# Expert tiles of 128 slots, two to a job, second weights kept in SBUF

## The reference, cut to what matters

```python
logits = einsum('btd,ed->bte', x, w_router); probs = softmax(logits)
vals, idx = top_k(probs, 2)                       # gates
hs  = gelu(x @ Ws1.T + bs1);  acc = hs @ Ws2.T + bs2       # shared
h   = gelu(einsum('btd,efd->btef', x, W1) + b1)            # 8 experts, F = 512
y   = einsum('btef,edf->bted', h, W2) + b2
out = SCALE * (acc + einsum('bted,bte->btd', y, gates))
```

## Time and profile before

| | us |
|---|---|
| median of 3 runs | 635.91 |
| lowest and highest run | 635.18, 636.79 |
| the profiled execution, its time | 635.87 |
| the profiled execution, its span | 634.1 |
| PE busy | 570.1 (90%) |
| DVE, ACT, POOL busy | 443.8, 333.6, 391.1 |

### The profile page before, as it was taken

One profiled execution on the slowest core, in us unless ns is written; L12 is line 12 of the kernel. 1 busy time (PEld: TensorE's weight loads), 2 busy tenths in 40 slices (PEclk: granted clock), 3 DMA queues, 4 the chain that ended last, 5 costly groups with the idle time before them and its releaser, 6 DMA issues. The chain is left out here.

```text
span 634.1 us, 14426 instructions
## 1 busy us (share of the span) xinstructions
PE 570.1 (90%) x4296; PEld 512.1 (81%) x4296; DVE 443.8 (70%) x1743; ACT 333.6 (53%) x1064; POOL 391.1 (62%) x598
## 2 busy tenths in 40 slices
PE   2469999999999999999996868789979999999993
PEld 2349999899999999999985557778869999999991
DVE  3736888888788888878886478884595465555765
ACT  2555666566566666656662374775434444444440
POOL 1525666656666665666652607888888886677760
PEclk9999999999999999999999768879999999999997
DMA  9079930000000000000000001145445577778945
GB/s 198 3 275 394 395 136 1 2 0 0 0 0 0 0 0 0 0 0 0 2 2 1 2 0 35 46 143 168 143 137 147 177 222 225 227 239 256 347 123 165
DMA packets 39796, 66.77 MB, mean 105 GB/s; under 512 B 7522, under 2 KB 26724, under 8 KB 39748
## 3 DMA queue, kind: packets, MB, share of 16 engines
q1 hardware_dynamic: 31076, 54.85, 27.4%
q0 software_dynamic: 4544, 9.45, 4.3%
q10 hardware_dynamic: 4128, 1.91, 1.4%
HBM read 36.26 MB, written 29.92 MB: 104 GB/s over the span
## 5 line engine op out<-in xcount | busy, mean ns | idle before, releaser
L1586 ACT ACTIVATE hid<-bank,slab 128x256 f32<-128x256 f32 x156 | 64.1, 470 | 85.1 <-PE bank L1442 85.0
L2052 POOL DMA_INDIRECT ys<-yo,dst x78 | 76.3, 979 | 36.8 <-DVE yo L1922 22.2
L2044 POOL DMA_INDIRECT xs<-hrow,slot_i x64 | 63.4, 990 | 35.8 <-issue 35.5
L1442 PE MATMUL bank<-hg,slab 128*128 128x256 f32 x312 | 73.9, 380 | 4.3 <-issue 3.9
L1456 PEld LDWEIGHTS bank<-slab,hid 128*128 128x128 f32 x624 | 75.8, 192 | 2.0
L1456 PE MATMUL bank<-slab,hid 128*128 128x128 f32 x624 | 76.0, 275 | 0.0
L1442 PEld LDWEIGHTS bank<-hg,slab 128*128 128x128 f32 x312 | 56.3, 190 | 11.0 <-issue 4.9
L1917 DVE TENSOR_TENSOR yb<-bank,slab 128x256 f32<-128x256 f32 x39 | 16.6, 424 | 61.9 <-PE bank L1456 61.7
L990 POOL TENSOR_TENSOR nL<-aL,ones 128x128 f32<-128x128 bf16 x32 | 16.9, 527 | 42.5 <-ACT aL L699 42.5
L413 PE MATMUL bank<-aH,W2p 128*128 128x128 f32 x192 | 42.4, 303 | 0.1
L413 PE MATMUL bank<-kv,W1b 128*128 128x128 f32 x192 | 41.4, 298 | 0.0
(11 more groups left out here) (353 smaller groups left out, 1882.4 us busy)
## 6 DMA issues: line engine op xcount, KB each, us to landing
slab<-in_slabs_dram SPq DMA_DIRECT2D x39, 578.0 KB, 3.8
xs<-fill SPq DMA_DIRECT2D x34, 528.0 KB
xt<-xs SPq DMA_DIRECT2D x39, 132.0 KB, 3.2
yg<-ys SPq DMA_DIRECT2D x8, 512.0 KB, 6.7
xr<-in_L_attn_x_dram SPq DMA_DIRECT2D x16, 128.0 KB, 7.0
ys<-yo,dst POOLq DMA_INDIRECT x78, 3.1
xs<-hrow,slot_i POOLq DMA_INDIRECT x64
out_dram<-xr SPq DMA_DIRECT2D x16, 64.0 KB, 2.9
```

The source lines that it names most:

```text
L1442: mm = pe.matmul(e_half(i, n), left[:, n * P:(n + 1) * P], right, start=True, stop=True)
L1586: nc.scalar.activation(hid[i % 2][:, n, :], e_half(i, n), ACT.Gelu_apprx_tanh, bias=bias).then_inc(e_x, 1)
L2044: pool.indirect_dma_start(out=xs[:, :], out_offset=bass.IndirectOffsetOnAxis(ap=slot_i[:, i, c:c + 1], axis=0), in_=hrow[:, c, :], in_offs ...
L2052: pool.indirect_dma_start(out=ys[:, :], out_offset=bass.IndirectOffsetOnAxis(ap=dst[v][:, s:s + 1], axis=0), in_=yo[v][:, s, :], in_offset ...
```

## The change

A tile has 128 slots (`HALF`), and a job takes two tiles that may belong to different experts. 64 full tiles and up to 7 part empty ones, made even, give 72 tiles or `N_TILES` = 36 jobs; `N_FULL` becomes 12. There are then 43 jobs in all: expert jobs 0 to 11 with four shared tiles among the first eight, a shared tile, expert jobs 12 to 35, two shared tiles. `e_up` has eight products of 128 columns instead of four of 256, and `e_gelu` eight pieces of 128. The second weights of all experts are loaded once (`w2`, 2 MB) and addressed in `e_down` through a register that TensorE loads itself. A slab has 644 numbers per partition and a job needs two; the ring is `RW` = 4. SyncE issues two slab DMAs and two row DMAs per job; it derives the expert from the row's register by a shift (an expert's region has 4096 rows), so a slab needs no register load of its own, except for the first ones (`early_weights`). `hid` shares the buffers of `hs`. The tables have 72 entries, and the grids behind them are finer.

```diff
-SLAB = 2 * F + FT + D
-N_TILES = (2 * B * S) // TS + E - 1
+SLAB = F + FT + D
+HALF = P
+N_HALVES = -(-((2 * B * S) // HALF + E - 1) // SUB) * SUB
+N_TILES = N_HALVES // SUB
-N_FULL = -(-(B * S - E * (TS - 1)) // TS)
+N_FULL = -(-(B * S - E * (HALF - 1)) // HALF) // SUB
-RW = 5
+RW = 4
@@ SyncE
-                def weights(j):
+                def weights(j, experts):
                     if j >= RW:
                         sp.wait_ge(e_yb, job["expert", j - RW] + 1)
-                    e = sp.value_load(e_i[0:1, j:j + 1], min_val=0, max_val=E - 1)
-                    sp.dma_start(slab[j % RW][:, :], slabs[:, bass.ds(e, 1), :].rearrange("p o w -> p (o w)")).then_inc(s_slab[j % RW], 16)
+                    for s in range(SUB):
+                        sp.dma_start(slab[j % RW][:, s, :], slabs[:, bass.ds(experts[s], 1), :].rearrange("p o w -> p (o w)")).then_inc(s_slab[j % RW], 16)
+                def early_weights(j):
+                    weights(j, [sp.value_load(e_i[0:1, SUB * j + s:SUB * j + s + 1], min_val=0, max_val=E - 1) for s in range(SUB)])
...
+                    at = [sp.value_load(row_i[0:1, SUB * j + s:SUB * j + s + 1], min_val=0, max_val=XS_ROWS - HALF) for s in range(SUB)]
+                    for s in range(SUB):
+                        sp.dma_start(xt[j % RX][:, s, :], xs[bass.ds(at[s], HALF), :]).then_inc(s_xt[j % RX], 16)
+                    return at
+                sp.dma_start(w2[:, :, :], e_w2).then_inc(s_w2, 16)
...
+                    at = rows(j)
                     if j >= RW:
-                        weights(j)
+                        weights(j, [a >> 12 for a in at])
                 sp.wait_ge(table_ready, 4)
-                weights(N_FULL)
-                weights(N_FULL + 1)
+                early_weights(N_FULL)
+                early_weights(N_FULL + 1)
@@ TensorE, e_up and e_down
+                        if kind == "expert":
+                            for s in range(SUB):
+                                mm = pe.matmul(e_half(i, n)[:, s * P:(s + 1) * P], slab[j % RW][:, s, n * P:(n + 1) * P],
+                                               hg[j % 2][:, s * P:(s + 1) * P], start=True, stop=True)
...
+                        expert = [pe.value_load(e_i[0:1, SUB * j + s:SUB * j + s + 1], min_val=0, max_val=E - 1) for s in range(SUB)]
...
-                            right = slab[j % RW][:, F + n * P:F + (n + 1) * P] if kind == "expert" else sw[:, 1, n, :]
+                            right = w2[:, bass.ds(expert[s], 1), n * P:(n + 1) * P].rearrange("p o w -> p (o w)") if kind == "expert" else sw[:, 1, n, :]
@@ DVE, meta
-                    dve.scalar_tensor_tensor(out=row2[:, :], in0=xt[r][:, :, D + 1], scalar=e, in1=xt[r][:, :, D],
-                                             op0=ALU.not_equal, op1=ALU.add)
+                    dve.tensor_tensor(other[:, :], xt[r][:, :, D + 1], etab[:, SUB * j:SUB * (j + 1)], ALU.not_equal).then_inc(meta_step, 1)
+                    dve.wait_ge(meta_step, 2 * j + 1)
+                    dve.tensor_tensor(row2[:, :], other[:, :], xt[r][:, :, D], ALU.add)
```

More of the change, by code:

```diff
@@ L132, in program @@
         at = 0
-        for name, width in (("iota", E), ("down", E), ("tri", E * E), ("step", CAP // TS), ("tile", N_TILES), ("tau", CH), ("dump", SUB * RY), ("b2row", D)):
+        for name, width in (("iota", E), ("down", E), ("tri", E * E), ("step", CAP // HALF), ("tile", N_HALVES), ("tau", CH), ("dump", SUB * RY), ("b2row", D)):
             cut[name] = tabs[:, at:at + width]
@@ L1215, in program @@
             held, marks = psb("held", [P, 3, E]), psb("marks", [P, 4 * E])
-            over = psb("over", [P, E, CAP // TS])
+            over = psb("over", [P, E, CAP // HALF])
             tri = psb("tri", [P, 3 * E, E])
-            past = psb("past", [P, N_FULL, E])
+            past = psb("past", [P, FULL, E])
             full, number, weight = psb("full", [P, E]), psb("number", [P, 3 * E]), psb("weight", [P, 3 * E])
-            first, rowf = psb("first", [P, N_TILES]), psb("rowf", [P, N_TILES])
+            first, rowf = psb("first", [P, N_HALVES]), psb("rowf", [P, N_HALVES])
             hs = [psb(f"hs{i}", [P, FT, SH]) for i in range(2)]
@@ L1223, in program @@
             xt = [psb(f"xt{i}", [P, SUB, ROW]) for i in range(RX)]
-            slab = [psb(f"slab{i}", [P, SLAB]) for i in range(RW)]
+            slab = [psb(f"slab{i}", [P, SUB, SLAB]) for i in range(RW)]
+            w2 = psb("w2", [P, E, F])
             hg = [psb(f"hg{i}", [P, TS]) for i in range(2)]
-            hid = [psb(f"hid{i}", [P, FT, TS]) for i in range(2)]
+            hid = hs
             yb = [psb(f"yb{i}", [P, SUB, D]) for i in range(2)]
@@ L1229, in program @@
             ysum = [psb(f"ysum{i}", [P, GRP, D]) for i in range(2)]
-            row2, rested = psb("row2", [P, SUB]), psb("rested", [P, 1408])
+            row2, other, rested = psb("row2", [P, SUB]), psb("other", [P, SUB]), psb("rested", [P, 1408])
             pause_done = sem("pause_done")
@@ L1249, in program @@
             s_yg = [sem(f"s_yg{i}") for i in range(NG)]
-            s_slab = [sem(f"s_slab{i}") for i in range(RW)]
+            s_slab, s_w2 = [sem(f"s_slab{i}") for i in range(RW)], sem("s_w2")
             meta_step, meta_ready = sem("meta_step"), sem("meta_ready")
@@ L1433, in e_up @@
                     if kind == "expert":
-                        pe.wait_ge(s_slab[j % RW], 16 * (j // RW + 1))
+                        pe.wait_ge(s_slab[j % RW], 16 * SUB * (j // RW + 1))
                         pe.wait_ge(e_hg, j + 1)
-                        left, right = slab[j % RW], hg[j % 2][:, :]
                     else:
@@ L1441, in e_up @@
                     for n in range(FT):
-                        mm = pe.matmul(e_half(i, n), left[:, n * P:(n + 1) * P], right, start=True, stop=True)
+                        if kind == "expert":
+                            for s in range(SUB):
+                                mm = pe.matmul(e_half(i, n)[:, s * P:(s + 1) * P], slab[j % RW][:, s, n * P:(n + 1) * P],
+                                               hg[j % 2][:, s * P:(s + 1) * P], start=True, stop=True)
+                        else:
+                            mm = pe.matmul(e_half(i, n), left[:, n * P:(n + 1) * P], right, start=True, stop=True)
                         if n % 2:
@@ L1448, in e_down @@
                     y = bank[4 + i % 2]
+                    if kind == "expert":
+                        if j == 0:
+                            pe.wait_ge(s_w2, 16)
+                            pe.wait_ge(table_ready, 2)
+                        if j == N_FULL:
+                            pe.wait_ge(table_ready, 4)
+                        expert = [pe.value_load(e_i[0:1, SUB * j + s:SUB * j + s + 1], min_val=0, max_val=E - 1) for s in range(SUB)]
                     if i >= 2:
@@ L1584, in e_gelu @@
                         act.wait_ge(e_u, 2 * i + n // 2 + 1)
-                        bias = slab[j % RW][:, 2 * F + n:2 * F + n + 1] if kind == "expert" else sb1[:, n:n + 1]
-                        nc.scalar.activation(hid[i % 2][:, n, :], e_half(i, n), ACT.Gelu_apprx_tanh, bias=bias).then_inc(e_x, 1)
+                        if kind == "expert":
+                            nc.scalar.activation(hid[i % 2][:, n, 0:P], e_half(i, n)[:, 0:P], ACT.Gelu_apprx_tanh,
+                                                 bias=slab[j % RW][:, 0, F + n:F + n + 1])
+                            nc.scalar.activation(hid[i % 2][:, n, P:TS], e_half(i, n)[:, P:TS], ACT.Gelu_apprx_tanh,
+                                                 bias=slab[j % RW][:, 1, F + n:F + n + 1]).then_inc(e_x, 1)
+                        else:
+                            nc.scalar.activation(hid[i % 2][:, n, :], e_half(i, n), ACT.Gelu_apprx_tanh, bias=sb1[:, n:n + 1]).then_inc(e_x, 1)
                 def to_exp():
@@ L1916, in e_post @@
                         v = j % RY
[L1917 removed]
+                        dve.tensor_tensor(yb[i % 2][:, :, :], y, slab[j % RW][:, :, F + FT:SLAB],
                                           ALU.add).then_inc(e_yb, 1)
```

72 lines of the change are left out of this document (34 added, 38 removed).

## The result

The kernel after takes 649.04 us (median of four runs, 646.35 to 652.24), the kernel before 635.97 in the same comparison: a ratio of 1.019, 95% interval 1.015 to 1.023 (the two medians alone would give 1.021, inside it). It is slower by 13 us, where 633.1 was forecast and 644 was the upper end of the range.

What follows compares the result with a forecast made beforehand. The prediction took the jobs to be bound by TensorE, busy in every window from 484 to 620. From 635.87 us, -11.2 + 2.2 + 1.2 + 0 + 2.5 + 1.0 + 1.5 = -2.8 gave 633.1 us, range 627 to 644.

Steps and rivals of the forecast that it cites:

- Three jobs: TensorE's path: 39 jobs become 36, at 3.73 us each, -11.2 us.
- pieces of 128: `e_up` on TensorE: 16 rows of 128 columns instead of 8 of 256, +0.06 us in each of 36 jobs, +2.2 us.
- GELU hidden: ACT: eight pieces of 128 columns take 2.86 us, below a job's 3.79, so 0.
- DVE's gaps: First jobs, ahead of two `e_up` that need `hg`: larger grids on DVE lengthen the waits, +1.2 us (bounds 0 and 2.2).
- passage: Change to the second half: job 12's rows stand behind `early_weights(13)`, so TensorE waits +2.5 us (bounds 1.0 and 3.5).
- One fall of the clock: Behind the second of the new gaps TensorE's clock falls once, +1.5 us (bounds 0 and 4).
- SyncE and the ring of 4: Steady jobs: SyncE needs 3.6 us a job, under 3.79; rows come in time by 0.6 to 1.6 us: 0.
- SyncE becomes the bound of the stage: Rival: SyncE takes 4.0 us a job, over 3.79, giving 644 us; case of SyncE or last jobs costing more: 0.24.
- TensorE's register loads: Two loads per expert job, 1.3 to 1.75 us, hidden by the sequencer's 2.0 us lead: 0.
- this rival: TensorE's loads uncovered at `L1469` in each expert job: 696 us, or 642 with a lead of 1.5 us; chance 0.13.
- The last jobs: Four `yg` loads share SyncE's queue, so late rows make TensorE wait, +1.0 us (bounds 0 and 6).
- The tail: The 14 us behind the last job stay as they are.

Runs made afterwards that it cites:

- e8: The kernel before with `e_up` and GELU of an expert job in pieces of 128 columns, nothing else: ratio 1.004 to before (1.001 to 1.008).
- e9: The kernel before once more, unchanged, as a control of the count of 0.7 us steps: 640.53 us against 639.72 of before.
- e5: The kernel after without the bound checks behind the register loads of SyncE and TensorE: ratio 1.009 to before (1.004 to 1.014).
- e1: The kernel after without TensorE's register loads, the second product taking a fixed expert's weights: ratio 1.015 to before (1.010 to 1.020).
- e14: The kernel after without bound checks, with rows and weights in pairs at the passage and five slab buffers: ratio 0.997 to before (0.994 to 1.000).
- e18: The kernel after with rows and weights in pairs at the passage and five slab buffers, all bound checks kept: ratio 1.013 to before (1.009 to 1.017).
- e3: The kernel after with rows and weights issued in pairs at the passage, without the two early weight loads: ratio 1.017 to before (1.014 to 1.021).
- e11: The kernel after with DVE's second table in nine pieces behind jobs 1 to 9 instead of four: ratio 1.020 to before (1.014 to 1.027).
- e13: The kernel after without bound checks and with rows and weights in pairs at the passage, ring of four: ratio 1.003 to before (1.001 to 1.006).
- e10: The kernel after without bound checks, with paired rows and weights at the passage, five slab buffers, DVE's second table in nine pieces: 635.80 us, ratio 0.995 to before.
- e7: The kernel before with two more, unused register loads on SyncE ahead of each row DMA: ratio 1.004 to before (1.001 to 1.008).

## Why the prediction was wrong

**The steps that held.** Three jobs -11.2, pieces of 128 +2.2 (e8: 2.8 us by its ratio, with an interval of 0.7 to 5), GELU hidden as long as nothing is late, DVE's gaps +1.2 (measured +2.0), passage +2.5 (3.2, for the reason given: rows behind six slab DMAs). One fall of the clock was forecast and there were two; that the first trace of before had none in the jobs was luck, as e9 shows, so +1.5 is near what the change itself adds.

**The step that failed** is "SyncE and the ring of 4 ... They come in time by 0.6 to 1.6 us: 0". It took a job's work of SyncE as a fixed sum, 3.6 us, and put it against 3.79. The sum was sound; undisturbed it is 3.3. But a queue at 87 to 95% of the bound has no room for what disturbs it, and I had no row of disturbances, as the one trace of before happened to have 8 steps where others have 32 and more. With them a job is 4.0 us. The other side of the comparison failed with it: the forecast gave the rows a lead of 7.58 - 3.8 = 3.8 us, and they have 2.0 to 3.2 in jobs 17 to 30; in e5, where SyncE has room, it is 2.9 to 4.1. So the rival "SyncE becomes the bound of the stage" is what happened, in a kernel whose ring had left it no lead to lose. I gave it 644 us and, with its neighbours, a chance of 0.24. Its price of 0.2 us a job was the right size (4.0 against 3.79), its cause was not: I had looked for it in the DMA issues, of which each still takes 0.33 us.

**"TensorE's register loads: 0"** was right for a job that is not disturbed, and wrong as a whole. The lead of 2.0 us is there: in 19 of the 36 jobs of the trace of after the first load starts 1.97 to 1.99 us ahead of its `e_down`. But from the first load to an `e_down` that follows as soon as it can it is 1.5 us (in the four jobs where it is shortest 1.50 to 1.53, three of which PE's waits above show as waits for `hs`), so a stop of the sequencer of over 0.5 us is paid by the array. That e1, without these loads, is at 1.015 puts their own price at some 0.4 to 0.7% by the medians, on a kernel whose rows are late anyway; the intervals overlap. By e14 and e18 the checks behind the loads of both engines cost 10 us once rows are in time. The forecast named this rival's place, and priced it with no cover (696 us) or with a lead short by 0.5 us in every job (642); it was covered until a train of steps and uncovered behind it. The page's rule weighed there, a floor of about 600 ns for a load (the Trainium skill, "DMA: Bandwidth & Descriptors", "Latency and other measured facts"), is not what these engines show: TensorE's 72 loads take

```profile
L1469 PEldq TENSOR_LOAD <-e_i x72: 296/302/454, 445.6 to 619.2; - x72
L1469 PEldq FUSED_REGOPS  x72: 146/151/156, 446.0 to 619.7; - x72
```

and it is the load with all that follows it that comes to 0.65 us.

**"The last jobs" +1.0** was 5.0: without lead each of them can be late. Three of the four late feeds are those of jobs 31, 33 and 34, behind `yg` loads, and there the rows are fed only 3.5 to 4.1 us after their issue, so the slower landings of the forecast have a part in it that no run separates. That the sum of the waits is what SyncE makes it, and not what each place asks for, is what e3 and e11 show, with one trace each: a wait taken away at one place comes back at the next.

**The tail** was put at no change and is 1.9 us longer in this trace, 0.6 in the second one of the kernel after (14.6 us against 14.0). In the chain after, the last scatter takes 3.67 us to land and the last `yg` load 5.12; before they took 2.42 and 4.73:

```profile
626.12 3.67 DMA ys<-yo,dst
...
630.86 5.12 DMA yg<-ys
```

e13 and e14 have nearly the tail of before (14.0 and 14.3), e10 doesn't (15.6). What decides it was not tried.

## What to carry to other kernels

A queue that issues another engine's data is to be costed with its waits, not with its work: read how long it still waits in a job and how far ahead of their use its data are issued, from more than one trace, as two traces of one kernel can differ by half of these waits. A thin margin did no harm while the lead was long (e7), and a short lead cost less while the margin was wide (e5, e13); the kernel after gave up both. Here no single wait behind such a queue was worth mending, since each was only moved; with room made on the queue first (by leaving out bound checks that the tables make needless), order and ring paid. And put a register load into a stream of matmuls only with its checks counted in.

## What the runs showed of the hardware that was not expected

- Steps of 0.70 us in SyncE's instruction stream, in trains, for any kind of instruction. Their count went from 8 to 68 between two executions of the same kernel. TensorE's sequencer stops with them: in e18 SyncE has trains from 522.7 to 524.8, 541.1 to 545.5, 558.3 to 562.0 and 574.0 to 578.4, and TensorE's sequencer, free to go on, stands still for 0.36 to 0.65 us and goes on at 525.5, 545.6, 562.0 and 578.4, as they end or just behind. That the two share what they wait for is likely; what it is, the supply of instructions or something else, stays open. Two readings narrow it. In e9 six trains in a row start at 520.7, 528.1, 536.2, 542.9, 550.4 and 557.8, on average 7.4 us apart, the time of two jobs, so they keep step with the program. And the two DMA queues that the profile calls instruction move the same in both traces of before, with 8 steps and with 68: 22 and 26 packets, 0.36 and 0.21 MB. So what differs is not how much they move. It also stays open whether the steps would be there in an execution that is not traced.
- A bound check behind a register load is not free: 0.15 us of register sum and an assertion of 18 ns, with the pauses 0.27 us of sequencer time, about as much as the load.
- A fall of the clock in the jobs lasts 3.4 us or twice that, half of which is lost. The four runs of after differ by 5.9 us and by 0.009 of mean clock, which is three to four such falls.
